# Cross attention of a decoder layer: the loop over batches 1 and 2 written out

## What is computed

```python
q = (x @ Wq).reshape(B, N, HEADS, hd).transpose(0, 2, 1, 3)
k = (context @ Wk).reshape(B, M, HEADS, hd).transpose(0, 2, 1, 3)
v = (context @ Wv).reshape(B, M, HEADS, hd).transpose(0, 2, 1, 3)
scores = jnp.einsum('bhid,bhjd->bhij', q, k) * scale
attn = jax.nn.softmax(scores, axis=-1)
out = jnp.einsum('bhij,bhjd->bhid', attn, v)
out = out.transpose(0, 2, 1, 3).reshape(B, N, DIM)
return out @ Wo
```

## Time and profile before

| what | us |
|---|---|
| median of 3 runs (lowest, highest) | 1402.81 (1402.61, 1403.64) |
| the profiled execution's own time | 1404.3 |
| its span, first to last instruction | 1402.2 |
| cross attention, first score product by context of batch 0 to the end of batch 3 | 631.5 to about 1110 |

### The profile page before, as it was taken

How to read it: one execution, slowest core, us unless ns; L and a number is a source line. 1 busy time by engine, 2 the same in 40 slices (tenths; PEclk the granted TensorE clock), 3 DMA queues, 4 the chain that set the end, 5 groups by cost and what they waited for, 6 DMA issues and landing times. The chain is left out here.

```text
span 1402.2 us, 21352 instructions
## 1 busy us (share of the span) xinstructions
PE 1238.2 (88%) x6678; PEld 742.9 (53%) x6679; DVE 986.9 (70%) x1769; ACT 629.1 (45%) x1174; POOL 279.6 (20%) x224
## 2 busy tenths in 40 slices
PE   6699999999999996769999999899999724999976
PEld 4478777877787776413343343334333212666655
DVE  3787787778788773677778768666888166666646
ACT  4233333333333332217677757665877621433432
POOL 1322222222222221001200200120000023555540
PEclk9899999999999999759999999999999966999998
DMA  5000000000000000562810660173130070111125
GB/s 195 0 1 1 1 1 1 1 2 1 1 1 1 1 0 25 147 129 50 153 25 7 110 116 1 30 121 60 58 124 1 0 219 19 58 60 54 58 74 155
DMA packets 61367, 72.39 MB, mean 52 GB/s; under 512 B 14472, under 2 KB 52744, under 8 KB 60632
## 3 DMA queue, kind: packets, MB, share of 16 engines
q1 hardware_dynamic: 53064, 56.58, 17.3%
q0 software_dynamic: 3792, 10.36, 2.4%
q10 hardware_dynamic: 4416, 4.20, 0.9%
HBM read 52.08 MB, written 18.78 MB: 51 GB/s over the span
## 5 line engine op out<-in xcount | busy, mean ns | idle before, releaser
L1318 DVE TENSOR_REDUCE neg_max<-pS 128x1 f32<-128x1024 f32 x256 | 306.8, 1220 | 72.1 <-PE pS L1025 70.3
L1178 ACT ACTIVATE pt<-pR 128x512 f32<-128x512 f32 x512 | 287.4, 601 | 101.9 <-PE pR L1047 95.2
L1047 PE MATMUL pR<-qs,ks 100*128 100x512 bf16 (+1 forms) x512 | 188.6, 386 | 9.0 <-issue 4.2
L1025 PE MATMUL pS<-ks,qs 100*128 (+1 forms) x512 | 162.2, 401 | 11.2 <-DMA qs<-q_scr 5.7
L1059 PE MATMUL b_pO<-pt,b_v 128*32 128x512 f32 x1024 | 137.3, 608 | 3.3 <-ACT pt L1178 2.7
L1047 PEld LDWEIGHTS pR<-qs,ks 100*128 100x128 bf16 (+1 forms) x512 | 49.3, 98 | 155.2 <-issue 75.7
L232 PE MATMUL pP<-w_feat,a_xT 128*128 128x512 f32 x256 | 123.1, 606 | 2.7 <-DVE kf L488 1.5
L171 POOL TENSOR_TENSOR kf<-kf,fsum 128x2048 f32<-128x2048 f32 x16 | 57.9, 3620 | 215.6 <-DVE fsum L498 215.6
L171 POOL TENSOR_TENSOR qf<-qf,fsum 128x2048 f32<-128x2048 f32 x16 | 58.8, 3673 | 184.7 <-DVE fsum L498 184.7
L290 PE MATMUL pO<-v,am 128*128 128x96 f32 x512 | 91.2, 275 | 0.0
L406 ACT COPY qfT<-pT 128x512 f32<-128x512 f32 x64 | 37.0, 579 | 116.0 <-PE pT L258 116.0
(11 more groups left out here) (295 smaller groups left out, 2136.1 us busy)
## 6 DMA issues: line engine op xcount, KB each, us to landing
k_scr<-parts SPq DMA_DIRECT2D x24, 256.0 KB, 2.8
qs<-q_scr SPq DMA_DIRECT2D x18, 256.0 KB
ks<-k_scr SPq DMA_DIRECT2D x6, 768.0 KB
ks<-in_L_ffn_w_dram SPq DMA_DIRECT2D x2, 2048.0 KB, 9.9
ks<-in_L_ffn_w_dram SPq DMA_DIRECT2D x4, 1024.0 KB, 11.4
c_y<-y_rows SPq DMA_DIRECT2D x16, 256.0 KB, 3.2
cx<-in_ctx_dram SPq DMA_DIRECT2D x4, 768.0 KB, 9.6
q_scr<-parts SPq DMA_DIRECT2D x12, 256.0 KB, 2.6
```

The costliest lines, as they stand in the source:

```text
L1025: ins = pe.matmul(pS1[:, slot, 512 * half:512 * half + 512], qs[0:KR, bass.ds(par, 1), h, P * t:P * t + P].rearrange("r a n -> r (a n)"), ...
L1047: pe.matmul(ring[bank], ks[0:KR, bass.ds(par, 1), h, P * j:P * j + P].rearrange("r a n -> r (a n)"), qs[0:KR, bass.ds(par, 1), h, :].rearr ...
L1178: nc.scalar.activation(pt[:, j % 2, i, :], ring[bank], ACT.Exp).then_inc(exp_done, 1)
L1318: nc.vector.tensor_reduce(neg_max[:, hg % 2, u // G, u % G:u % G + 1], pS1[:, u % 2, :], AX_X, ALU.max, negate=True).then_inc(max_done, 1)
```

## The change

The four `Fori(1, B - 1)` become Python loops over b = 1 and 2, and two conditions in ACT's `small` are rewritten so that they ask for the number b rather than for its type; they choose the same semaphores and counts. Linear attention's loops and the experts' loops stay as they are, and SP's program too.

```diff
--- before.py
+++ after.py
@@ -950,7 +950,7 @@
                                 n += 1
 
                 batch(0, START, True)
-                with pool.Fori(1, B - 1) as b:
+                for b in range(1, B - 1):
                     batch(b, steps_before(b), False)
 
             @block.tensor
@@ -1110,7 +1110,7 @@
                     return start + n
 
                 batch(0, START, True, False)
-                with pe.Fori(1, B - 1) as b:
+                for b in range(1, B - 1):
                     batch(b, steps_before(b), False, False)
                 n = batch(B - 1, steps_before(B - 1), False, True)
                 weighted_values(B - 1, G - 1, JT - 1)
@@ -1137,16 +1137,16 @@
                                        pM[:, :].rearrange("c (t k n) -> c t k n", t=2, k=2)
                                        ).then_inc(emptied, 1)
                     elif kind == "k":
-                        if i // 2 and not (isinstance(b, int) and b == 0):
+                        if i // 2 and b:
                             wait(act, stored[2], 48 * (b + 1))
-                        elif isinstance(b, int) and b == 1:
+                        elif b == 1:
                             wait(act, stored[2], 48)
-                        elif not isinstance(b, int):
+                        elif b:
                             wait(act, stored[1], 48 * b)
                         nc.scalar.copy(parts[:, slot(b, kind, i), 0, i % 2, :].rearrange("p a n -> p (a n)"),
                                        pM[:, :]).then_inc(head_done, 1)
                     elif kind == "q":
-                        if isinstance(b, int):
+                        if b < 2:
                             wait(act, stored[b], 48)
                         else:
                             wait(act, stored[0], 48 * b)
@@ -1206,7 +1206,7 @@
                     return start + n
 
                 batch(0, START, True, False)
-                with act.Fori(1, B - 1) as b:
+                for b in range(1, B - 1):
                     batch(b, steps_before(b), False, False)
                 n = batch(B - 1, steps_before(B - 1), False, True)
                 values_copy(NG)
@@ -1395,7 +1395,7 @@
                 own = Chain(dve, s_dve, before)
                 batch(0, START, True, False, own)
                 assert own.n == OWN_FIRST, own.n
-                with dve.Fori(1, B - 1) as b:
+                for b in range(1, B - 1):
                     own = owned(b)
                     batch(b, steps_before(b), False, False, own)
                     assert own.n == OWN_MIDDLE, own.n
```

## The result

| | before | after |
|---|---|---|
| median of 15 runs each, us (lowest to highest) | 1401.84 (1399.28 to 1405.97) | 1393.91 (1391.40 to 1401.96) |
| the profiled executions' spans, us | 1402.2 | 1396.4 |
| first score product by context to the start of the last, us | 476.5 | 468.1 |

The ratio is 0.9949, with a 95% interval of 0.9934 to 0.9964: 7.1 us off 1401.84, between 5.0 and 9.2 (the two medians of the table lie 7.9 apart). The prediction was 7.2 off, and 1395.6.

A forecast was written before the change was run, and what follows sets the result against it. PE was taken to set the pace, so gains come from its idle and low-clock time. 4.45 + 1.69 + 1.74 + 0.6 - 0.3 - 1.0 = 7.2 us off the median 1402.81: 1395.6 us, range 1391.3 to 1399.5.

The forecast's parts named there:

- PE's jump back, (3,7) of batch 1: Cross attention, end of batch 1: step takes 7.73 us looped, 3.28 in straight batch 0; 4.45 us gained, all taken as gone.
- the clock behind it, (0,0) of batch 2: First step after PE's idle time at the branch: granted clock averages 0.51, 5.13 us against 3.44; 1.69 us gained.
- (0,3) to (0,7), two batches: Steps where PE waits for ACT and DVE, whose register instructions stand in the chain; 0.45 + 0.42 a batch, 1.74 us gained.
- (0,0) to (0,2) and (1,7), no twin: Steps without a straight counterpart having the same small steps; 0.3 us a batch assumed, 0.6 gained, bounds 0 and 0.9.
- (0,7) to (1,6), two batches: 28.99 us straight against 28.84 looped: straight code 0.15 us slower per batch, 0.3 lost.
- m_turn at (1,6), two batches: DVE's four short operations meet POOL twice and end 0.71 us later; 0.5 a batch, 1.0 us lost, bounds 0 and 1.4.
- (2,0) to (3,7), two batches: 52.14 us straight, 52.13 looped: register instructions cost nothing; a change there would mean they did more than shown.
- the clock at (1,6) and (1,7): Second clock drop in each looped batch, worth 1.65 us; left where it is because the two waits before it remain.
- no drop: Rival at (1,6): waits fall differently, both clock drops vanish, worth 1.65 us each; 1392.3 us, chance 0.17.
- a longer one: Rival at (1,6): longer m_turn wait, clock drop covers twice as much, 1.7 us more lost per batch; 1399.0, chance 0.12.
- The rivals at the seam: Straight code also stops for code: 1401.7 us, chance 0.05; or experts' loop jumps miss: 1421.2 us, chance 0.04.
- the last rival: Experts' loop on PE: moved addresses make its seven jumps cost 3.87 us, not 0.215; 25.6 us slower, 1421.2, chance 0.04.

## Why the prediction was right, and where not

| term of the sum | forecast, us | profile after |
|---|---|---|
| PE's jump back, (3,7) of batch 1 | +4.45 | 7.73 to 3.18: +4.55 |
| the clock behind it, (0,0) of batch 2 | +1.69 | 5.13 to 3.45: +1.68 |
| (0,3) to (0,7), two batches | +1.74 | +1.74 |
| (0,0) to (0,2) and (1,7), no twin | +0.6 | 0 at full clock; -0.1 in (0,1) and (0,2) of batch 2 |
| (0,7) to (1,6), two batches | -0.3 | +0.47 |
| m_turn at (1,6), two batches | -1.0 | -1.0 at full clock |
| (2,0) to (3,7), two batches | 0 | +0.32 |
| (3,7) of batch 2 | 0 | +0.27 |
| the clock at (1,6) and (1,7) | 0 | +0.4: 1.7 gained in batch 1, 1.3 lost in batch 2 |
| sum | 7.2 | 8.3 |

The two large terms were right in mechanism and in size. That 7.2 meets the 7.1 of the runs to 0.1 us is luck beyond that: the interval is 2 us to either side, the batches give 8.3 in the first pair of profiles and 7.8 in the second, the small terms were off by up to 0.8 us both ways, and the clock at (1,6), taken as unchanged, moved by over 1 us in each batch with opposite signs.

*The jump.* Right, and shown by both halves: it returns with PE's loop, goes with PE's loop, and a short jump in its place costs nothing. That the time is the fetching of code is well supported. The twelve profiles hold twelve long jumps of PE in the two stages, of 3.34 to 3.87 us, and in each a 16 KB packet of the queue that brings PE's code starts 0.9 to 1.5 us into the branch and lands 1.36 to 1.53 us before its end (before: packet 878.0 to 879.0, branch 876.5 to 880.4). The branch is as long as the packet is late and slow. About the short jump no such packet comes within 11 us. What fills the last 1.4 us stays open.

*The clock behind it.* Right in size, 5.13 and 5.22 us in the two profiles of the kernel before, and it appears with PE's jump in every one of the three profiles that have it. The size is not fixed: with PE alone looped the step took 6.20.

*Register instructions.* The step that they cost only where PE waits for ACT and DVE is confirmed: (0,3) to (0,5) is 9.10 with PE looped and 9.47 with PE straight. Other engines' register instructions, not PE's, made that time. The 0.6 us for the steps without a twin was a guess and came to nothing: no run shows it. The 0.16 us by which (1,7) of batch 1 fell, 4.72 to 4.56, was the end of the clock drop; where that drop stayed away, in batch 2 of the second profile of before, the looped step takes 4.56 too.

*(0,7) to (1,6).* Wrong in sign. I took batch 0 as the twin, 28.99 against 28.84, and charged 0.15 a batch; written out, batch 1 takes 28.65. In the changed kernel, all straight, batch 0 and batch 1 differ in the first step of the stretch alone, (0,7), 3.61 against 3.27 us: batch 0 comes from a step (0,6) in which m_turn is the last small step, without the `oT` behind it. So the pair was the mistake: batch 0 carried 0.34 us of its own, which hid 0.19 of register instructions, at (1,2) and (1,5). (2,0) to (3,7) was misread the same way: 52.14 against 52.13 looked like no cost, but batch 0's (2,0) takes 4.73 where batch 1's takes 4.56, and written out batch 1 takes 51.97, 0.16 less than looped. The prediction had named a change there as a sign that the register instructions did more than the pairs show, and so it was. Equal names of small steps inside a stretch don't make it a twin; the step ahead of it must be the same as well.

*Step (1,6).* Right, though it goes against first sight: the straight code is later there. m_turn was forecast 0.71 us later and came at 4.12 in place of 3.41, the step costs 8.06 against 7.54 with PE alone straight, 0.52 against 0.5 forecast, and POOL's work is the cause, shown by taking it away and again by moving it ahead. One remark was wrong: PE does hang on m_turn in batch 0 as well, where the smaller POOL operations made (1,6) 1.3 us and (1,7) 0.35 us shorter.

*The clock at (1,6).* I left the two drops where they were, one in each batch. In the profile after there is one, of 6.8 us. Against before, batch 1 gains 1.0 over the step and batch 2 loses 1.8 over (1,6) and (1,7), the later m_turn included. My first two rivals, no drop and a longer one, each came true in one batch, and they nearly cancel. That the drop is not tied to a batch was shown; what decides when it comes was not. Over the profiles: with the waits of straight code, 2.1 and about 1 us, it fell in one batch of two in each of five profiles (batch 2 four times, batch 1 once); with the shorter waits of looped code, 1.38 and 1.09, in three of six batches; with a wait of 0.46, or with `y` 0 moved away, in none of eight.

*The rivals at the seam.* Straight code did not stop for its code, and the experts' loop lost nothing: 7 taken jumps at 0.215 us in the median, as before. How many lines of code PE holds, on which the last rival turned, no run shows.

*ACT's jump* was passed over: I wrote that its seam costs nothing by itself. It costs 1.1 us as soon as PE no longer stands there. Since all four loops were written out at once, the sum did not show it.

## What to carry to other kernels

A loop with a long body can cost a stall at each jump back: here 3.3 to 3.9 us on PE, whose two long bodies had some 1700 and 1800 instructions by the trace, 2.4 to 2.6 us on ACT with some 340, and 2.8 to 3.1 us on DVE with some 330 in the linear attention; DVE with some 250 and ACT with some 150 went on within 0.3 us, and PE with some 220 took 0.2 us. It counts on the critical path only by what the products already issued don't cover, and the clock of TensorE fell behind it in the cross attention, where PE stood idle for 4 us, and not in the linear attention, where it stood for 0.8. Price it at the step that holds it, against the same step where the program runs straight, and look at which engine's loop it is: writing out PE's alone gave here what all four gave, within the 2 us that these runs resolve.

When waits disappear from an engine, its operations move, and may land beside another engine's: in a chain of four dependent DVE operations of 0.2 us, each that started within one of POOL's lasted until POOL's ended, 1.0 us, two of the four in straight code and one in looped. Keep such a chain away from the split that precedes it; moving three small steps to free places took the ratio from 0.9945 to 0.9862, some 12 us, more than the change itself.

## What the runs showed that I had not expected

The same two waits of PE, 2.1 and about 1 us, within one step, went with a granted clock of 0.5 for 0, 3.4 or 6.8 us in otherwise equal batches, worth 0 to 2.9 us each time. Much the same branch, 3.8 to 3.9 us, cost 4.55 us in one stage and 1.0 in the other.
